# A decoder layer's cross attention: 256-column results in a PSUM bank of their own, head outputs in one bank instead of two

## What is computed

```python
def _L0_xattn_ref(x, latents, mask, g1, b1, g2, b2, Wq, Wkv, Wout):
    heads, dim_head = (16, 64)
    xn = layer_norm(x, g1, b1)               # the context, 512 rows a batch
    ln_lat = layer_norm(latents, g2, b2)     # the tokens, 256 rows a batch
    q = ln_lat @ Wq
    kv = jnp.concatenate([xn, ln_lat], axis=1) @ Wkv      # 768 keys a batch
    k, v = jnp.split(kv, 2, axis=-1)
    q, k, v = (to_heads(q), to_heads(k), to_heads(v))
    weight = jnp.einsum('bhld,bhnd->bhln', q * scale, k * scale)
    weight = jnp.where(full_mask[:, None, None, :], weight, neg)
    weight = jax.nn.softmax(weight.astype(jnp.float32), axis=-1).astype(q.dtype)
    out = jnp.einsum('bhln,bhnd->bhld', weight, v)
    out = out.transpose(0, 2, 1, 3).reshape(b, l, heads * dim_head)
    return out @ Wout
```

## Time and profile before

| | us |
|---|---|
| Three runs | 1219.43, 1220.61, 1220.95 (median 1220.61) |
| The profiled execution's own time, first to last instruction (its span) | 1221.5 |
| Cross attention in it | 226.0 to 1014.6, together 788.6 |
| PE matmuls busy in the span | 1123.2 (92%) |
| DVE busy | 879.1 (72%) |
| ACT busy | 755.0 (62%) |
| POOL busy | 418.3 (34%) |

### The profile page before, as it was taken

One profiled execution on the slowest core, in us unless ns is written; L12 is line 12 of the kernel. 1 busy time (PEld: TensorE's weight loads), 2 busy tenths in 40 slices (PEclk: granted clock), 3 DMA queues, 4 the chain that ended last, 5 costly groups with the idle time before them and its releaser, 6 DMA issues. The chain is left out here.

```text
span 1221.5 us, 29151 instructions
## 1 busy us (share of the span) xinstructions
PE 1123.2 (92%) x8775; PEld 967.0 (79%) x8775; DVE 879.1 (72%) x2777; ACT 755.0 (62%) x1779; POOL 418.3 (34%) x453
## 2 busy tenths in 40 slices
PE   2998898399999999989999989999999986899996
PEld 2877777278888888878888878888888866899996
DVE  3998897687777787867787857787876755555555
ACT  2998997377666766756776756776766754222222
POOL 4554453134433434433433432533433424000000
PEclk9999999699999999999999999999999996899998
DMA  5000021000000000000000000000000000000001
GB/s 172 7 6 5 5 87 40 1 1 1 1 2 1 2 2 2 1 4 2 2 2 1 2 4 2 1 1 1 2 2 1 2 1 1 1 1 0 0 1 35
DMA packets 11403, 12.31 MB, mean 10 GB/s; under 512 B 1152, under 2 KB 9344, under 8 KB 11136
## 3 DMA queue, kind: packets, MB, share of 16 engines
q1 hardware_dynamic: 8032, 5.90, 1.7%
q10 hardware_dynamic: 3232, 4.73, 1.2%
HBM read 9.57 MB, written 1.05 MB: 9 GB/s over the span
## 5 line engine op out<-in xcount | busy, mean ns | idle before, releaser
L803 POOL TENSOR_TENSOR xk_parts<-k_raw,xk_parts 64x768 fp32r<-64x768 f32 x128 | 236.5, 1848 | 444.2 <-DVE xk_parts L895 444.2
L919 DVE CUSTOM_DVE_ANT_0 xmasked<-ps,bar 128x768 f32<-128x768 f32 x256 | 244.2, 954 | 6.0 <-issue 1.6
L852 ACT ACTIVATE xprobs<-xmasked,xlow 128x768 f32<-128x768 f32 x256 | 238.1, 930 | 6.1 <-issue 5.3
L999 PE MATMUL ps<-xk_parts,xq_parts 128*128 128x512 f32 (+1 forms) x1024 | 232.9, 349 | 4.5 <-DVE xq_parts L900 2.7
L1005 PE MATMUL ps<-ident,xprobs 128*128 128x128 f32 x1536 | 215.0, 276 | 1.5 <-DVE xprobs_t L924 1.1
L999 PEld LDWEIGHTS ps<-xk_parts,xq_parts 128*128 128x128 f32 x1024 | 175.1, 190 | 28.9 <-DVE xq_parts L900 3.2
L1016 PE MATMUL ps<-xprobs_t,xvals 128*64 128x256 f32 x1536 | 179.9, 383 | 1.1 <-ACT xprobs_t L858 1.1
L1005 PEld LDWEIGHTS ps<-ident,xprobs 128*128 128x128 f32 x1536 | 169.3, 140 | 9.4 <-DVE xprobs_t L924 1.3
L1016 PEld LDWEIGHTS ps<-xprobs_t,xvals 128*64 128x64 f32 x1536 | 104.7, 137 | 57.9 <-issue 10.5
L924 DVE COPY xprobs_t<-ps 128x768 f32<-128x768 f32 x128 | 121.6, 950 | 4.5 <-PE ps L1005 4.5
L112 DVE MEMSET xspare<- 128x1 f32 x256 | 15.1, 59 | 148.5 <-PE ps L999 114.6
(11 more groups left out here) (183 smaller groups left out, 2395.4 us busy)
## 6 DMA issues: line engine op xcount, KB each, us to landing
w_up<-in_L_ffn_w SPq DMA_DIRECT2D x2, 1024.0 KB, 6.8
raw_kv<-in_L_xattn_Wkv ACTq DMA_DIRECT2D x1, 1024.0 KB, 5.3
x_in<-in_x SPq DMA_DIRECT2D x8, 128.0 KB, 2.2
out<-state SPq DMA_DIRECT2D x4, 256.0 KB, 2.6
raw_q<-in_L_xattn_Wq ACTq DMA_DIRECT2D x1, 512.0 KB, 6.6
keep_all<-in_mask_BxS_bk ACTq DMA_DIRECT2D x1, 512.0 KB, 14.0
wout<-in_L_xattn_Wout ACTq DMA_DIRECT2D x1, 512.0 KB, 6.7
w_up<-in_L_ffn_sw SPq DMA_DIRECT2D x2, 128.0 KB, 4.0
```

The source lines that it names most:

```text
L803: pool.tensor_tensor(k_parts[dst, i // 2 % 2, h, :], k_raw[src, :], k_parts[src, i // 2 % 2, h, :].bitcast(F32), ALU.subtract).then_inc(k_ ...
L852: nc.scalar.activation(probs[:, i % 4, :], masked[:, i % 4, :], ACT.Exp, scale=-1.0, bias=low[:, i % 4:i % 4 + 1], accum_out=sums[:, pair ...
L919: dve.tensor_tensor_reduce(masked[:, i % 4, :], slot(slots.place("S", i), KEYS), bar[:, par, :], 1.0, 3e38, ALU.add, ALU.min, low[:, i % 4 ...
L999: last = nc.tensor.matmul(slot(s, hi - lo, lo), q_parts[:, pair % 2, h, part, t * P:(t + 1) * P], k_parts[:, pair % 2, h, lo:hi], start=pa ...
```

## The change

The results of 256 columns (Q, R, TX, OUT) leave the ring of three double banks. They share one bank, bank 6, and each waits until the reader of the one just before it has finished. The ring is left to TC, K, V, S and PT. The head outputs of all pairs go to bank 7, so that PV of pair n waits for NORM of pair n-1 instead of n-2.

```diff
-    slots = Turns(pe_order, full, SLOTS)
+    NARROW = ("Q", "R", "TX", "OUT")
+    wide = Turns(pe_order, [k for k in full if k not in NARROW], SLOTS)
+    narrow = Turns(pe_order, NARROW, 1)
+    NARROW_BANK, HEADS_BANK = O_BANK, O_BANK + 1
+
+    def narrow_bank(n, at=0):
+        return ps[:, NARROW_BANK, at:at + n]
...
# DVE, NORM
-                    dve.tensor_tensor(heads_t[:, i, :], ps[:, O_BANK + i % 2, 0:S], rsum_t[:, i % 2, :],
+                    dve.tensor_tensor(heads_t[:, i, :], ps[:, HEADS_BANK, 0:S], rsum_t[:, i % 2, :],
                                       ALU.mult).then_inc(heads_ready, 1)
...
# PE
                 if kind in full:
-                    s = slots.place(kind, i)
-                    earlier = slots.before(kind, b, i)
+                    turns = narrow if kind in NARROW else wide
+                    s = turns.place(kind, i)
+                    earlier = turns.before(kind, b, i)
                     if earlier:
                         wait(pe, *taken(*earlier))
...
# PE, PV
-                    wait(pe, heads_ready, n - 1)
+                    wait(pe, heads_ready, n)
...
-                            last = nc.tensor.matmul(ps[h * XD:(h + 1) * XD, O_BANK + i % 2, 0:S],
+                            last = nc.tensor.matmul(ps[h * XD:(h + 1) * XD, HEADS_BANK, 0:S],
...
```

More of the change, by code:

```diff
@@ L21 @@
 from contextlib import ExitStack
+from functools import partial
 import concourse.bass as bass
@@ L826, in emit @@
                     lo, hi, g, ready = {"TC": (0, C, 0, yc_ready), "TX": (C, KEYS, 2, yx_ready)}[kind]
-                    nc.scalar.activation(y[:, lo:hi], slot(slots.place(kind, 0), hi - lo), ACT.Identity,
+                    nc.scalar.activation(y[:, lo:hi], (narrow_bank(hi - lo) if kind == "TX" else slot(wide.place(kind, 0), hi - lo)), ACT.Identity,
                                          scale=gb[:, g:g + 1], bias=gb[:, g + 1:g + 2]).then_inc(ready, 1)
@@ L831, in emit @@
                     wait(act, k_ready, b * XH + 2 * i)
-                    nc.scalar.activation(k_raw[:, :], slot(slots.place("K", i), KEYS), ACT.Copy).then_inc(k_out, 1)
+                    nc.scalar.activation(k_raw[:, :], slot(wide.place("K", i), KEYS), ACT.Copy).then_inc(k_out, 1)
                 if kind == "Q":
@@ L837, in emit @@
                         rows = slice(h * XD, (h + 1) * XD)
-                        nc.scalar.activation(q_parts[rows, i % 2, h, 0, :], slot(slots.place("Q", i), S)[rows, :],
+                        nc.scalar.activation(q_parts[rows, i % 2, h, 0, :], narrow_bank(S)[rows, :],
                                              ACT.Copy, scale=Q_SCALE).then_inc(q_hi_done, 1)
@@ L844, in emit @@
                     nc.scalar.activation(vals[:, i // 2 % 2, half, :].rearrange("p k c -> p (k c)"),
-                                         slot(slots.place("V", i), KT // 2 * 4 * XD), ACT.Copy).then_inc(v_ready, 1)
+                                         slot(wide.place("V", i), KT // 2 * 4 * XD), ACT.Copy).then_inc(v_ready, 1)
                 if kind == "EXP":
@@ L858, in emit @@
                     nc.scalar.activation(probs_t[:, i % 4, :, 0, :],
-                                         slot(slots.place("PT", 2 * i), KEYS).rearrange("p (k t) -> p k t", k=KT),
+                                         slot(wide.place("PT", 2 * i), KEYS).rearrange("p (k t) -> p k t", k=KT),
                                          ACT.Copy).then_inc(pt_act, 1)
@@ L863, in emit @@
                     wait(act, heads_ready, b * PAIRS + i - 1)
-                    nc.scalar.activation(rsum_t[:, i % 2, :], slot(slots.place("R", i), S), ACT.Copy).then_inc(rsum_t_ready, 1)
+                    nc.scalar.activation(rsum_t[:, i % 2, :], narrow_bank(S), ACT.Copy).then_inc(rsum_t_ready, 1)
             act_order.run(act, emit, 2)
@@ L900, in emit @@
                         dve.scalar_tensor_tensor(out=q_parts[rows, i % 2, h, 1, :],
-                                                 in0=slot(slots.place("Q", i), S)[rows, :], scalar=Q_SCALE,
+                                                 in0=narrow_bank(S)[rows, :], scalar=Q_SCALE,
                                                  in1=q_parts[rows, i % 2, h, 0, :].bitcast(F32),
@@ L918, in emit @@
                     hold(dve, spare[:, i % 4:i % 4 + 1])
-                    dve.tensor_tensor_reduce(masked[:, i % 4, :], slot(slots.place("S", i), KEYS), bar[:, par, :], 1.0, 3e38,
+                    dve.tensor_tensor_reduce(masked[:, i % 4, :], slot(wide.place("S", i), KEYS), bar[:, par, :], 1.0, 3e38,
                                              ALU.add, ALU.min, low[:, i % 4:i % 4 + 1]).then_inc(masked_ready, 1)
@@ L924, in emit @@
                     dve.tensor_copy(probs_t[:, i % 4, :, 1, :],
-                                    slot(slots.place("PT", 2 * i + 1), KEYS).rearrange("p (k t) -> p k t", k=KT)
+                                    slot(wide.place("PT", 2 * i + 1), KEYS).rearrange("p (k t) -> p k t", k=KT)
                                     ).then_inc(pt_dve, 1)
@@ L942, in emit @@
                     tokens = state[:, bass.ds(b * T, T), :]
-                    dve.tensor_tensor(tokens, slot(slots.place("OUT", 0), T * D).rearrange("p (t d) -> p t d", t=T), tokens,
+                    dve.tensor_tensor(tokens, narrow_bank(T * D).rearrange("p (t d) -> p t d", t=T), tokens,
                                       ALU.add).then_inc(added, 1)
@@ L963, in emit @@
                     for n, j in enumerate(range(CT) if kind == "TC" else range(CT, KT)):
-                        last = nc.tensor.transpose(slot(s, P, n * P), normed[:, j, :], ident[:, :])
+                        last = nc.tensor.transpose((narrow_bank if kind == "TX" else partial(slot, s))(P, n * P), normed[:, j, :], ident[:, :])
                     last.then_inc(full[kind], 1)
@@ L977, in emit @@
                     wh, wl = (a[:, i * P:(i + 1) * P] for a in (m.wq_hi, m.wq_lo))
-                    nc.tensor.matmul(slot(s, S), wh, y_hi[:, par, C:KEYS], start=True, stop=False)
-                    nc.tensor.matmul(slot(s, S), wh, y_lo[:, par, C:KEYS], start=False, stop=False)
-                    nc.tensor.matmul(slot(s, S), wl, y_hi[:, par, C:KEYS], start=False, stop=True
+                    nc.tensor.matmul(narrow_bank(S), wh, y_hi[:, par, C:KEYS], start=True, stop=False)
+                    nc.tensor.matmul(narrow_bank(S), wh, y_lo[:, par, C:KEYS], start=False, stop=False)
+                    nc.tensor.matmul(narrow_bank(S), wl, y_hi[:, par, C:KEYS], start=False, stop=True
                                      ).then_inc(full["Q"], 1)
@@ L1023, in emit @@
                     for j in range(T):
-                        last = nc.tensor.transpose(slot(s, P, j * P),
+                        last = nc.tensor.transpose(narrow_bank(P, j * P),
                                                    rsum_wide[:, i % 2, j, :, :].rearrange("p h c -> p (h c)"), ident[:, :])
@@ L1030, in emit @@
                         for pair in range(PAIRS):
-                            last = nc.tensor.matmul(slot(s, D, t * D), heads_t[:, pair, t * P:(t + 1) * P],
+                            last = nc.tensor.matmul(narrow_bank(D, t * D), heads_t[:, pair, t * P:(t + 1) * P],
                                                     m.wout[:, pair, :], start=(pair == 0), stop=(pair == PAIRS - 1))
```

## The result

| | us |
|---|---|
| Before, 4 runs | 1219.43 to 1220.95, median 1220.12 |
| Changed, 4 runs | 1259.27 to 1260.36, median 1259.94 |
| Ratio | 1.0324, 95% interval 1.0309 to 1.0339 |
| Forecast | 1259.9, range 1252 to 1270 |

The changed kernel is 39.8 us slower (the median of before has one more run in it than the three given ahead). The profiled executions differ by less (1257.4 after, 1221.5 before). The stage explains all of it: from the first weight load of PV to the last it takes 748.9 us before and 789.4 after, 40.5 more. Outside the stage the profiled execution after is 4.1 us shorter, 2.1 ahead of it and 2.0 behind. The change doesn't touch that code, and the stretches at half clock fall differently there: one of 3.4 us less ahead of the stage, and 29 us in place of 38 behind it.

A forecast was written before the change was run, and what follows sets the result against it. PE was taken to set the cross attention stage, busy 97% of it. PV's wait 34.7 plus TX's 5.6 minus the ring's 1 made 39.3 us, on the median of 1220.6 giving 1259.9 us; range 1252 to 1270.

The forecast's parts named there:

- PV behind NORM: Cross attention, 63 pairs: PE's PV waits for the previous pair's NORM, queued behind the mask on DVE; 34.7 us added.
- TX behind OUT: Six seams between batches: TX waits for DVE's addition of OUT, 0.93 us each, 5.6 us added.
- The other new waits at nothing: R behind Q's low part, Q behind R's copy, OUT behind ACT's copy of R: all covered, taken as nothing.
- What the deeper ring gives back: PE's listed waits on ring banks in the stage total 4.2 us; gain taken as 1 us, between 0 and 4.2.
- The waits met in time: Rival, 3%: PV and TX find their banks empty after the first pairs, only the deeper ring's gain is left; 1216.4 us.
- The clock: Rival, 5%: new pauses drop PE's granted clock to half; 1270 us if once per seam, 1367 if once per pair.
- DVE behind in every pair: Rival, 3%: all pairs become like the third of a batch, 61.3 us added, 1281.9 us.

The follow-up runs named there:

- the heads' bank alone: Kernel before with only the head outputs of all pairs in one bank, PV waiting for the previous pair's NORM; ring as before: 1257.36 us against 1220.97.
- NORM early and TX late: Changed kernel with NORM due 9.1 instead of 9.25 on DVE, and TX due -25.5 on PE and -24.7 on ACT instead of -26: 1213.94 us.
- the dose: Changed kernel with NORM due 10.1 instead of 9.25, behind both halves of Q's low part on DVE: 1392.51 us, ratio 1.1413.

## Why the prediction was right

The mechanism was right, and so was the time, but that it came so close is luck: misses of up to 4 us cancel. The sizes below are from the traces, from the first pair's PV to the last one's, one execution of each kernel; the run with the heads' bank alone serves to tell PV's term from the rest. By the steps:

- **PV behind NORM, 34.7 us forecast.** The distances were right (30.4 us in sum), their place and their 63 occurrences too, and that PE can't make them up. The signal was too small: 0.116 a time instead of 0.07, as in this kernel the wait sits on a semaphore instruction ahead of the load; in the earlier trace rows it sat on the load. In the earlier trace rows such an instruction stood ahead of the load too, and it was still 0.07 us: there it had waited since 1003.75 for the copy, the second of its two semaphores, while in the changed kernel NORM's, the first, comes last. 30.4 + 63 x 0.116 = 37.7, and a steady pair is 0.03 us longer than distance and signal make it. With the heads' bank alone the traces give 38.8 without what the turns of the loop cost over steady pairs, under my upper bound of 39.8.
- **TX behind OUT, 5.6 us.** The six seams are 5.7 us longer than with the heads' bank alone.
- **The other new waits at nothing.** Right but for the start of the stage: none of those named stands in the list.
- **What the deeper ring gives back, 1 us, at most 4.2.** In the changed kernel it is some 1.7 us, most of it in the first pair. But the reasoning was wrong, and shows once PV's pause is gone: with NORM early and TX late the ring is worth 7.0 us. I took the list of waits as the whole of what the ring costs. It leaves out pauses of a tenth of a microsecond, of which each pair had one.
- **What the sum left out.** PE's pauses at the two turns of the loop, with what follows them, took 11.7 us over steady pairs in the trace before and 9.4 in the trace after, 2.3 less. Whether the change does this or they vary from run to run was not tested.
- **The sum.** 38.8 + 5.7 - 1.7 - 2.3 = 40.5, as the traces show; the medians give 39.8, and the forecast was 39.3. PV's term was 4.1 short, and what the ring gives back and the turns, 0.7 and 2.3, stand against it.
- **Rivals.** The waits met in time (1216.4): not here, but moving NORM by 0.15 units brought nearly that about (1219.0, and 1213.9 with TX late). The clock: not in the changed kernel, but real in the dose, with its longer pauses. The Trainium skill's rule ("TensorE: Matmul & The Clock Gate", "A second HAM failure mode: psum-queue depth-cycling") has frequent short pauses swing the clock; 62 pauses of up to 1.5 us, 0.7 in the mean, didn't, and some of those of the dose, 2.3 to 3.9 us, did. DVE behind in every pair: no.

Open: why a turn of the loop stops PE for 3.1 us in one trace and 4.7 in another was not settled, only that both pauses go with the turns.

## What to carry to other kernels

Before two users share a bank, find the reader that frees it and count what stands ahead of that reader on its own engine; if it is work that needs PE's latest result, the bank can come free too late, and moving the reader up by one step can be worth as much as a second bank (1219.0 us with one bank and NORM early, 1221.0 with two and NORM late, 1219.5 with two and NORM early). A list of waits has a floor: a wait of 0.1 us that repeats in every round shows only in the distance of two starts, and one removed may turn up at the next use of the ring. Take the time of a signal from a place where the same kind of instruction waits, and for the same semaphore as the last.

## What the runs showed of the hardware

From the end of a VectorE instruction to the start of a waiting TensorE weight load it was 0.054 us if the load waited itself, 0.116 with one semaphore instruction between and 0.212 with a register instruction ahead of that. With one semaphore instruction between that waited for two semaphores and had the other already, it was 0.07 (once in the kernel before). That the order in which four waits are written moves a kernel by 3.3 to 5.2 us (0.3 to 0.4%) was not expected. Nor was it that the granted clock stands a pause in each of 62 pairs (0.7 us in the mean, 1.5 at most). With pauses of 2.4 us in the mean it fell to half for 3.4 us at a time in 13 more places: behind each of the six pauses of 3.9 us, and at seven of 2.3 to 2.4 us.
